# Local attention in chunks of 32 queries and 64 keys, one softmax step per pair of heads, in 64x64 tiles of TensorE

## What is computed

```python
def attn_layer(x, Wqkv, qs, ksc, Wo):            # x already token-shifted
    q, k, v = split(x @ Wqkv)                    # 16 heads of 64
    q, k = l2norm(q) * qs, l2norm(k) * ksc
    q, k = rotary(q, scale), rotary(k, 1 / scale)
    # windows of 32: a query sees its own window and the one before it,
    # keys j with i - 32 <= j <= i
    sim = einsum('bhwie,bhwje->bhwij', bq, bk2) * 8.0
    sim = where(mask, -max, sim)
    out = einsum('bhwij,bhwje->bhwie', softmax(sim, -1), bv2)
    return out @ Wo
for i in range(6):
    x = attn_layer(shift_tokens(x), ...) + x
    x = ffn_layer(shift_tokens(x), ...) + x      # layernorm, 128 -> 2 x 341, gelu gate, -> 128
```

## Time and profile before

| | |
|---|---|
| median of 3 runs | 5675.37 us (5674.71 to 5675.73) |
| the profiled execution | 5674.6 us, span 5672.5 us |
| mean granted clock | 0.96 |
| PE busy | 5156.9 us, 91% of the span, 68706 matmuls |
| DVE, ACT, POOL busy | 4207.5, 4014.1, 2657.0 us |
| DMA | 89.14 MB, mean 16 GB/s |

### The profile page before, as it was taken

How to read it: one execution, slowest core, us unless ns; L and a number is a source line. 1 busy time by engine, 2 the same in 40 slices (tenths; PEclk the granted TensorE clock), 3 DMA queues, 4 the chain that set the end, 5 groups by cost and what they waited for, 6 DMA issues and landing times. The chain is left out here.

```text
span 5672.5 us, 176489 instructions
## 1 busy us (share of the span) xinstructions
PE 5156.9 (91%) x68706; PEld 3769.0 (66%) x68706; DVE 4207.5 (74%) x6500; ACT 4014.1 (71%) x7192; POOL 2657.0 (47%) x2485
## 2 busy tenths in 40 slices
PE   8997995799999999999998899799999999999998
PEld 3334432587777777777776433687777777777776
DVE  7885655687777777777776788687777777777775
ACT  5784664577777777777776578677777777777775
POOL 1100100465566665566654110475656665656663
PEclk8996997899999999999999899899999999999999
DMA  0000000100000000000000000100000000000000
GB/s 13 2 2 6 2 2 9 35 20 15 19 17 18 21 17 20 16 21 19 17 21 13 4 2 2 37 19 16 20 18 16 23 16 21 15 21 17 17 22 18
DMA packets 129243, 89.14 MB, mean 16 GB/s; under 512 B 33396, under 2 KB 122000, under 8 KB 128376
## 3 DMA queue, kind: packets, MB, share of 16 engines
q1 hardware_dynamic: 128376, 77.32, 4.9%
HBM read 69.54 MB, written 1.05 MB: 12 GB/s over the span
## 5 line engine op out<-in xcount | busy, mean ns | idle before, releaser
L1746 POOL TENSOR_TENSOR cross<-raw,tab_b 128x512 f32<-128x512 f32 x768 | 998.5, 1324 | 298.8 <-ACT raw L1612 295.5
L737 DVE TENSOR_REDUCE arena<-PS 128x1 f32<-128x512 f32 (+3 forms) x1408 | 828.9, 648 | 215.9 <-PE PS L550 130.4
L1752 POOL CAST kT_b<-kT 128x512 bf16<-128x512 f32 x384 | 349.5, 910 | 1199.2 <-ACT kT L1668 1198.1
L688 ACT ACTIVATE arena<-PS 128x1024 f32<-128x1024 f32 (+1 forms) x704 | 668.8, 968 | 200.7 <-PE PS L573 124.2
L1838 DVE TENSOR_TENSOR rot<-PS,tab_a 128x512 f32<-128x512 f32 x768 | 522.7, 687 | 330.7 <-ACT raw L1612 172.0
L1612 ACT COPY raw<-PS 128x512 f32<-128x512 f32 x768 | 448.1, 592 | 270.2 <-PE PS L1463 224.1
L1861 DVE TENSOR_TENSOR rot<-rot,inv_norm 128x1024 f32<-128x1024 f32 x384 | 561.8, 1463 | 47.7 <-ACT inv_norm L1628 37.8
L1867 DVE TENSOR_TENSOR oT<-PS,rec_den 128x384 f32<-128x384 f32 (+1 forms) x576 | 298.8, 519 | 369.3 <-ACT rec_den L1646 369.0
L1854 DVE TENSOR_TENSOR rot<-rot,cross 128x1024 f32<-128x1024 f32 x384 | 560.0, 1458 | 14.9 <-POOL cross L1746 13.7
L1442 PE MATMUL PS<-PT,V 128*64 128x96 f32 x8448 | 484.4, 256 | 76.2 <-DVE oT L1867 60.6
L1463 PE MATMUL PS<-w_qk_high,x_high 128*128 128x256 f32 x1536 | 478.0, 311 | 79.0 <-issue 34.0
(11 more groups left out here) (260 smaller groups left out, 12668.8 us busy)
## 6 DMA issues: line engine op xcount, KB each, us to landing
w_qk<-in_w_pairs SPq DMA_DIRECT2D x196, 128.0 KB, 2.1
w_v<-in_w_pairs SPq DMA_DIRECT2D x100, 128.0 KB, 2.2
w_o<-in_w_out_pairs SPq DMA_DIRECT2D x192, 64.0 KB, 1.9
xs<-staged SPq DMA_DIRECT2D x24, 224.0 KB, 2.5
w<-in_L_ffn_W SPq DMA_DIRECT2D x12, 341.0 KB
q_parts<-max_rows SPq DMA_DIRECT2D x192, 2.0 KB
V<-in_c_E SPq DMA_DIRECT2D x2, 896.0 KB, 7.9
w<-in_L_ffn_W SPq DMA_DIRECT2D x24, 64.0 KB
```

Source lines behind the costliest of these rows:

```text
L688: nc.scalar.activation(PT[u % 6].rearrange("p (a n) -> p a n", a=2)[:, :, first_q:512], PS[:, 2 * (u % 2):2 * (u % 2) + 2, first_q:512], A ...
L737: nc.vector.tensor_reduce(maxima[:, 2 * m + h, qt, kh:kh + 1], bank[:, 0:keys_of(qt, kh)], AX.X, ALU.max).then_inc(bank_free, 1)
L1746: nc.gpsimd.tensor_tensor(dst[:, :, :, o:o + 32], src[:, :, :, other:other + 32], tab[:, :, o:o + 32].unsqueeze(2).broadcast_to([128, 8, 2 ...
```

## The change

- Chunks are 32 queries by 64 keys, so that every chunk sees exactly its own window and the one before; 32 chunks. Four chunks make a unit of 128 tokens (8 units): chunk 4m + 2w + t stands in the row half w of the tiles' outputs and in the column half t of its 64 columns of the bank. Scores of one head fill one bank (8 x 64 columns), and the pair has one step: `scores`, `exps`, `values`, `denominators` and `quotients` are called once per position, 1024 wide over two banks.
- Mask and maxima, scores, values and the sums with ones are all in 64x64 tiles. The sums go to banks 4 and 5 once the scores are read, the values to 6 and 7. `values` comes after slots 1 and 2, nothing of it is left to the next position.
- `maximum` takes 64 queries by 96 keys, 8 units for 11 chunks; all maxima stand in one `max_parts`, turned by one product. Its constant columns come from a small table in DRAM.
- V is projected for 8 units instead of 11 chunks, four fills V0 to V3. Chunks with t = 0 need keys that start 32 earlier, so SP copies V, shifted by 32 partitions, into `V_early` by two DMAs inside SBUF (96 partitions x 8 KB, 32 x 7 KB) in every even p, behind its wait for V3, and `values` waits for them (`v_moved`) in odd p.
- PT, log_den, rec_den, R and max_parts have one buffer each.

```diff
-                values_of = {0: {0: [0], 5: [1], 1: [2, 3], 3: [4, 5]}, 7: {}}.get(p, {5: [0], 3: [1]} if p % 2 else {0: [2], 5: [3], 1: [4], 3: [5]})
+                values_of = {0: {0: [0], 5: [1], 1: [2], 3: [3]}, 7: {}}.get(p, {5: [0]} if p % 2 else {0: [1], 5: [2], 1: [3]})
...
+                            taken_apart(sp, l, b, p, "V3")
+                            need_apart(sp, pv_full, it - 2)
+                            sp.dma_start(V_early[j % 2][32:128, :, :], V[j % 2][0:96, :, :]).then_inc(v_moved, 16)
+                            sp.dma_start(V_early[j % 2][0:32, 1:UNITS, :], V[j % 2][96:128, 0:UNITS - 1, :]).then_inc(v_moved, 16)
...
+                def scores(l, b, p, r):
                     par = (p + 1) % 2
+                    need(pe, rows_made, r + 1)
...
+                    for m in range(UNITS):
                         for w in range(2):
                             for h in range(2):
+                                rows = slice(64 * h, 64 * h + 64)
+                                nc.tensor.matmul(PS[64 * w:64 * w + 64, 4 + h, 64 * m:64 * m + 64], E[rows, UNITS if (m, w) == (0, 0) else m, :],
+                                                 R[rows, 64 * w:64 * w + 64], start=m == 0, stop=True, tile_position=(64 * h, 64 * w), skip_group_check=True)
+                    for m in range(UNITS):
+                        for t in range(2):
+                            for w in range(2):
+                                for h in range(2):
+                                    rows, at = slice(64 * h, 64 * h + 64), 128 * m + 64 * w + QC * t
+                                    last = nc.tensor.matmul(PS[64 * w:64 * w + 64, 4 + h, 64 * m + QC * t:64 * m + QC * t + QC], kT[par][rows, at:at + 64],
+                                                            qT[par][rows, at:at + QC], start=False, stop=True,
+                                                            tile_position=(64 * h, 64 * w), skip_group_check=True)
                     last.then_inc(st_full, 1)
...
+                def values(l, b, p, r):
+                    pair = (p + 7) % 8
+                    need(pe, exp_done, r + 1)
+                    need(pe, o_done, r)
+                    if p % 2 == 1:
+                        need(pe, v_moved, (r + 2) * 16)
...
+                    for m in range(UNITS):
+                        for t in range(2):
+                            for w in range(2):
+                                for h in range(2):
+                                    rows, at, to = slice(64 * w, 64 * w + 64), 128 * (pair % 2) + 64 * h, 64 * m + QC * t
+                                    nc.tensor.matmul(PS[64 * h:64 * h + 64, 6 + w, to:to + QC], (V_early, V)[t][pair // 2 % 2][rows, m, at:at + 64],
+                                                     PT[rows, h, to:to + QC], start=True, stop=True, tile_position=(64 * w, 64 * h), skip_group_check=True)
+                    for w in range(2):
                         for h in range(2):
+                            rows = slice(64 * w, 64 * w + 64)
+                            last = nc.tensor.matmul(PS[64 * h:64 * h + 64, 4 + w, :], ones[rows, 0:64], PT[rows, h, :], start=True, stop=True,
+                                                    tile_position=(64 * w, 64 * h), skip_group_check=True)
                     last.then_inc(pv_full, 1)
...
                     if bb:
-                        scores(l, b, p, r, 0)
+                        scores(l, b, p, r)
                     late(l, b, p, 1)
-                    for s in range(NS - 1):
...
+                    late(l, b, p, 2)
+                    if bb:
...
+                        values(l, b, p, r)
+                    late(l, b, p, 3)
                     late(l, b, p, 4)
```

More of the change, by code:

```diff
@@ L1166, in window_layers @@
         ff_cols, b2_row = own("ff_cols", [128, 8]), own("b2_row", [128, C])
[L1167 to L1170, removed]
+        E = own("E", [128, UNITS + 1, 64], BF16)
+        half_mask = [own(f"half_mask{m}", [128, 5, KB], BF16) for m in range(2)]
+        R, max_parts = own("R", [128, 128], BF16), own("max_parts", [128, 128], BF16)
         norms2 = [own(f"norms2_{m}", [128, 16]) for m in range(2)]
@@ L1400, in maximum @@
                     last.then_inc(full, 2)
-                def scores(l, b, p, r, s):
-                    chunks = STEPS[s]
+                def scores(l, b, p, r):
                     par = (p + 1) % 2
-                    if s == 0:
-                        need(pe, rows_made, r + 1)
-                    need(pe, exp_done, r * NS + s)
-                    for i, c in enumerate(chunks):
-                        g = int(c in GROUPS[1])
-                        for h in range(2):
-                            e = 12 + h if c == 0 else 6 * h + c - GROUPS[g][0]
-                            nc.tensor.matmul(PS[:, 4 + h, QC * i:QC * i + QC], E[:, e, :], R[:, g, :], start=i == 0, stop=True,
-                                             skip_group_check=True)
-                    for i, c in enumerate(chunks):
+                    need(pe, rows_made, r + 1)
+                    if not isinstance(l, int):
+                        pe.sem_inc(passed, 1)
+                    for m in range(UNITS):
@@ L1432, in second_batch @@
                     pe.wait_ge(zeroed, ZEROED)
[L1433 to L1446 removed]
+                    pe.wait_ge(consts_made, 4)
@@ L1705, in position @@
                     if bb:
-                        exps(r, 0)
+                        exps(r)
                     if a:
@@ L1709, in position @@
                     late(l, b, p, 1)
-                    for s in range(NS - 1):
-                        if bb:
-                            exps(r, s + 1)
-                            denominators(r, s)
-                        if a and s == 0:
-                            inverse_norm(l, b, p, 1)
-                        late(l, b, p, s + 2)
+                    if a:
+                        inverse_norm(l, b, p, 1)
+                    late(l, b, p, 2)
+                    if bb:
+                        denominators(r)
+                    late(l, b, p, 3)
                     late(l, b, p, 4)
@@ L1785, in position @@
                         if p % 2 == 0:
-                            need(pool, full, fill(l, b, p, "V5") + 1)
+                            need(pool, full, fill(l, b, p, "V3") + 1)
                             split_v(phi * 4 + (4 + p // 2 + 1))
@@ L1948, in position @@
                         add_sine(l, b, p, 1)
+                        normalise(l, b, p, 1)
+                    late(l, b, p, 2)
                     if bb:
-                        quotients(r, 0, (p + 1) % 2)
-                    if a:
-                        normalise(l, b, p, 1)
-                    for s in range(1, NS):
-                        late(l, b, p, s + 1)
-                        if bb and s < NS - 1:
-                            quotients(r, s, (p + 1) % 2)
+                        quotients(r, (p + 1) % 2)
+                    late(l, b, p, 3)
                     late(l, b, p, 4)
```

180 lines of the change are left out of this document (72 added, 108 removed).

## The result

The changed kernel takes 5901.97 us in the median of 4 runs (5898.31 to 5906.70) where the kernel before takes 5675.55 (4 runs): a ratio of 1.0397, 95% interval 1.038 to 1.0413. It is slower by 226 us, and the forecast of 5470 us was wrong by 430 us and in its sign. The profiled execution took 5901.9 us, span 5900.1, mean granted clock 0.921 (0.96 before), PE busy 4838.5 us for 5156.9.

What follows compares the result with a forecast made beforehand. TensorE sets the pace, DVE and ACT 20% behind. Positions gain 10.6 us a batch, less 1.8 for the clock: 22 batches at 8.8 and two at 5 save 204 us, giving 5470 us, range 5290 to 5640.

Steps and rivals of the forecast that it cites:

- an fp32 round of four tiles at 58 ns: PE's scores and values: a round of 32-column products takes 58 ns, so 32 rounds take 1.86 us.
- p=1: Odd position of a batch: sum of PE's parts 18.1 us for 19.3 before, a gain of 1.2.
- p=2: Even position of a batch: 17.0 us for 17.2 before, a gain of 0.2, as K0/q0 waits for DVE.
- rival 1: fp32 rounds in scores and values: short ones cost what long ones do, 90 ns, giving 5805 us; chance 0.14.
- The move: V's shifted copy inside SBUF by DMA: taken as 8 us, in time for the odd position's values, costing nothing.
- the term for instructions: Two more `passed` increments and the setup loads: 0 to 0.1 us, hidden by the queue ahead of the array; taken as 0.
- PE's 3.0 us less per position: PE's work on scores, values, V projection and maxima: 3.0 us less per position, 570 us in sum.
- The clock: TensorE's clock falling after holes: between 0 and 6 us a batch, taken as 1.8.
- Rival 2: TensorE's clock falls after most holes: 4.2 us more per batch, 100 us, giving 5570 us; chance 0.15.
- the two normalised halves on DVE end first: 2.1: p=3: of 23.5 us PE idles 3.4, but DVE's normalised halves end first, so the gain is 2.1 us.
- The hole itself: PE out of work before the second maximum: Q0's start to Q2's takes 4.85 us, for some 4.0 before.
- slower: Outcome of the whole kernel being slower than before: chance 0.14, resting on short fp32 rounds costing what long ones do.

Runs made afterwards that it cites:

- experiment 7: Kernel before, each fp32 score product of 96 columns cut into three of 32: 5968.3 us, ratio 1.0502.
- experiment 9: Changed kernel with the order of 4 and the two rstd operations of p=2 behind the copies of K1 and q1: 5699.8 us.
- 4: Changed kernel with denominators behind the next position's first two raw copies on ACT, quotients behind its maxima on DVE: 5723.5 us.
- 10: Kernel of experiment 9 with slot 1's work between the halves of the scores and the second square ahead of the exponential: 5677.7 us.
- 11: Kernel of 10 with V's slot 3 fill between the halves of p=0's values and slot 5's between those of p=4's scores: 5637.0 us.

## Why the prediction was wrong

*Right.* PE's part: V by 24 products; an fp32 round of four tiles at 58 ns (128 products of L1423 start within 1.9 us, and experiment 7 was priced by it); log_den 1.027 us; scores 2.27 us from mask to next work where nothing breaks them, for 2.3, and values with their sums 2.96 for 2.95; p=1 at 18.6 undisturbed for 18.1, p=2 at 16.4 for 17.0. In all 542 us of 570. So rival 1 didn't come, and the Trainium skill's floor of 25 ns from start to start ("TensorE: Matmul & The Clock Gate", section "Wait — 56ns, not 53.3ns?") doesn't hold for tiles: here four start within 58 ns. The move landed in 5.6 to 5.9 us for 8 taken and never made `values` wait.

*The step that failed first* is the term for instructions. PE's 3.0 us less per position were right as work, but were turned into time with no look at how the instructions get there: "The two more `passed` increments and the setup loads: 0 to 0.1 us" was all that I charged for 21600 more products and as many weight loads. None of my rivals had it. The profile of before had the sign: its queue q8 moves 576 packets of 16 KB, and no burst of its PE passes 256 instructions in under 6 us, while I planned one of 32 + 128 products with their loads in 2.3 us. Cost: 182 us of stalls, and part of the clock.

*The clock* was the second: I took 1.8 us a batch between 0 and 6. Measured it is 9.2 (221 us over 24 batches). Rival 2 had the mechanism and 100 us; the holes came in all positions, and with stalls between them, which it didn't have. The Trainium skill describes such a case (same page, section "A second HAM failure mode: psum-queue depth-cycling"): short idle times between groups of products make the clock swing, and the loss is in falling and warming up again. This trace agrees, with 120 stretches; the forecast had weighed each hole by itself.

*The order* of the queues was the third, in "the two normalised halves on DVE end first: 2.1" and the like. The least p=3 is 24.4 us for 21.4 forecast, p=4 23.9 for 22.2, p=5 22.2 for 20.6. The hole itself was forecast too long where nothing disturbs it: from Q0's start to Q2's p=6 and p=7 take 3.7 us, for 4.85 forecast and 3.9 before. In p=3 the same way takes 7.1 us in the mean, for 5.3 before, as I had put the quotients at 3.5 us, ahead of raw 0, but neither the bn_aggr behind them nor rstd behind these; with both out of the way (experiment 9) it is 4.4. The least positions sum to 169.0 us, 1.7 under the kernel before, not 10.6; but those of p=0, 3 and 4 still hold a stall or a stretch at 1.2 GHz, and without these, 5.2 us at most, it would be 163.8. So 3.7 to 8.9 us a batch, 90 to 215 us, were missing in the chains themselves. The experiments are in line with this: order alone (4 and 9) took back 202 of the 430 us, a good part of it by way of the clock; the two that also break bursts (10 and 11) took back 63 more.

*The range* ended at 5640, 262 us short of the result; "slower" had 0.14, by a mechanism that didn't act.

Open: what PE's 1.4 us behind a packet's landing are, and why some packets start late with no move in flight. No run parts the clock's share in a stall from the stall's own, nor the shares of stalls, clock and order in the 430 us: each experiment moves more than one of them.

## What to carry to other kernels

Count instructions as well as their durations: products that start every 15 ns come with a weight load each, and a burst of some 300 instructions in 2 us outran their supply here, though each product was as fast as hoped. Break such a burst with long products that something already waits for, and first move ahead what hangs on its end. When steps are merged, write down for each engine what stands behind the merged operation: with the same products, the order on the queues (202 us) and long products inside the bursts, with the second square moved ahead of the exponential (63 us), decided here between +4.0% and -0.7%.

## What the runs showed of the hardware that I had not expected

- PE's instructions come in packets of 256 (16 KB) during the run, and the borders lie at fixed places of the program: 64 semaphore increments ahead of a loop moved the stalls by 32 products. On PE's instruction queue, q8, 736 such packets go by during an execution.
- Such a border cost 0.3 to 3 us where PE's instructions went by fast or their packet started late, and PE went on 1.2 to 1.6 us behind the packet's landing; where no 256 instructions went by in under 3.1 us (experiment 7) the stalls together cost 2.6 us.
- Short fp32 products in four tiles keep 58 ns a round with 64 x 64 weights, at 32 columns.
